# Two-layer Mamba, attention and experts kernel: another order of the start-up, one wider bias product, and a new table of half slots for layer 1

## The chip, the cores and the metric

The kernel runs on one core of a Trainium2 chip. The core has five engines with an instruction stream each: TensorE (PE), VectorE (DVE), ScalarE (ACT), GpSimd (POOL) and SyncE (SP), which mostly issues DMAs. They wait for each other through semaphores. The metric is the device time of one execution in microseconds (us); lower is better.

## The reference, cut to what matters

The input x is 32 sequences of 256 tokens with 128 features, float32. Two layers follow, each of the form x = x + attn(layernorm(x)) + ffn(layernorm(x)).

```python
# layer 0, attn: a Mamba block
xi, z = split(rmsnorm(xn, rms_w) @ in_proj)          # 128 -> 2 x 256
xi = silu(causal_conv4(xi, conv_w) + conv_b)
dt, Bm, Cm = split(xi @ x_proj)                      # 8, 16, 16
delta = softplus(dt @ dt_w + dt_b)                   # (tokens, 256)
h = exp(delta * A) * h + (delta * xi) * Bm           # scan over 256 tokens, 16 states
y = (sum(h * Cm) + xi * D) * silu(z);  attn = y @ out_proj
# layer 0, ffn: 8 experts, all computed, gated by top-p (0.8)
ffn = sum_e gate_e * (relu(xn @ W1[e] + b1[e]) @ W2[e] + b2[e])
# layer 1, attn: 16 heads, latent width 64, head width 8, rotary halves, causal softmax
q, k, v = ((xn @ W_down) per head) @ W_up;  attn = softmax(q k^T / sqrt(8)) v @ Wc
# layer 1, ffn: 128 experts, top 2, 32 places per expert, first come first served
```

## The kernel before, in words

Layer 0 (`layer0()`) works on 16 blocks of 512 tokens, each of 4 tiles of 128 tokens. A block is written as 32 half slots, h = 0 to 31, and every engine runs the same generic loop, `pipeline()` (L205). In each half slot an engine does the pieces of the current block (`slot`) and the pieces that prepare the next one (`fore`). Which `fore` piece stands in which half slot is read from a table for each engine (`PE_AT`, `ACT_AT` and so on, L181 to L187).

The pieces of the current block are these. ACT computes dA = exp(delta*A) (L555) from replicas of delta, which SP loads from DRAM into REP. POOL computes dBx (L685) from replicas of delta*x and of B (BC). DVE scans (L845) and multiplies with C (L854), and PE adds up the states (L395). Beside it PE computes the experts' up products (L374, bank UP) and down products (L383, bank DN); ACT applies relu (L564) and the gate (L571), and POOL sums (FF, L695). At the end of a block `output()` makes the experts' bias term (L405, from gT and b2) and the output projection (L407) in the bank FRO.

The pieces that prepare a block are XN and XQ on POOL (L734 to L742), the transposes (L442), the two conv halves x0 and x1 (L447, L451, then ACT L611, DVE L914), xproj (L458), the two halves of the delta input (L467, then ACT L597, L598), softplus (ACT L638, L642, L646; DVE L923, L933; POOL L751, L755), dx (POOL L762), the router (L479 and after) and z (L488). All of them use the one bank FRO. SP stores the results to the scratch tensors s_b, s_delta and s_dx and loads them back 32-fold (L261, L266).

Before block 0 the same pieces run alone, in one pass over 32 half slots (the prologue). There `between(s)` adds, once per slot of two half slots, the statistics of the remaining tiles of x (DVE L820), the products that combine layer 1's W_down and W_up (`project(n, part)`, n = q, k, v: PE L357 transposes and L362 products, ACT L527 to L537 copies), and, at its end, the layer norm of the other 60 tiles (`norms(OTHERS)`, DVE L993 to L1020 and L799 to L806, with two square roots on ACT, each of which loads a table). On SP the loads are issued in the order of the code: x (L244), 24 small loads (L248), x in six pieces (L251), four stores of a constant (L254), XI (L297), the experts' W (L314), the 21 loads for `project` (L316), b2 (L318).

Layer 1 (`layer1()`) is attention and the 128-expert part in one pipeline over the 32 sequences. A sequence has 12 half slots; `schedule()` puts each piece at its half slot 12n + at, or further ahead for the routing pieces (`ahead`), by the tables `PE_AT` to `SP_AT` (L1125 to L1129). The scores are computed twice: p1 (L1298 to L1310) gives row maxima (DVE `mx`, L1748), and p2 (L1320 to L1332) gives what ACT exponentiates (L1504); pv (L1346, L1348) multiplies with V. SP's `load` (L1208) issues 12 DMAs, KS and then QS, for the next sequence; it waits until p2 has read the old QS and until the parts of that sequence are stored. The routing pieces are g (L1387), `top` (DVE L1677, L1680), `mk`, `count` (L1401, L1402; ACT copy CS), `loc` (DVE L1694), `oh`, `val` and `map` (L1408). The output pieces are ot (L1448), `epi` (DVE L1731, L1733), yt (L1453), yT (ACT L1493) and wc (L1458). xnt (L1368) transposes the normed x, and xT (ACT L1477) copies it out.

Of the kernel before, what the change touches and what calls it, by code (L numbers as in the profile page):

```python
# [9 lines left out]
ALU = mybir.AluOpType  # L10
# [3 lines left out]
P = 128  # L14
# [36 lines left out]
def layer0(nc, ctx, t, dram, scratch):  # L51
# [19 lines left out]
    def sem(name):  # L71
# [3 lines left out]
    XC, XT = 6, (NT - J0) // 6  # L75
# [58 lines left out]
    wloaded = sem("wloaded"); dloaded = sem("dloaded"); wT = sem("wT"); wTc = sem("wTc"); wE = sem("wE"); stat_step2 = sem("stat_step2")  # L134
    root_done2 = sem("root_done2"); loaded = sem("loaded"); xloaded = [sem(f"xloaded{i}") for i in range(XC + 1)]; zeroed = sem("zeroed"); stat_step = sem("stat_step")
# [18 lines left out]
    a_log = dram["L0_attn_A_log"].rearrange("(b d) s -> d b s", d=CB)
# [3 lines left out]
    for h in range(HALF):  # L158

        rows = xproj[:, h, 0:2 * S].rearrange("p (a c q) -> p a c q", c=2, q=2)  # L160
        for c in range(2):
            loads.append((rows[:, :, c, :], xp[:, h, RANK + S * c:RANK + S * c + S].rearrange("p (a q) -> p a q", q=2)))
        loads.append((xproj[:, h, DT_AT:DT_AT + RANK], xp[:, h, 0:RANK]))
    wloads = [
# [11 lines left out]
    dloads = [(WD[:, n, :], dram[f"L1_attn_W{k}_down"]) for n, k in enumerate("qkv")]  # L176
# [11 lines left out]
    FIRST, OTHERS = slice(0, J0), slice(J0, NT)  # L188
    STATS_END = 2 * XC
    PROJ0 = 8  # L190
# [14 lines left out]
    def pipeline(fore, start, slot, end, eng, between=lambda s: None):  # L205
# [19 lines left out]
        start()  # L225
# [7 lines left out]
        end(IT0 - 1, 1)  # L233

# [7 lines left out]
    def _(sp):  # L242
        xd = tokens(dram["L0_attn_x"].rearrange("b t d -> (b t) d"))
        sp.dma_start(X0[:, 0:J0, :], xd[:, 0:J0, :]).then_inc(xloaded[0], 16)  # L244

        sp.wait_ge(zeroed, 1)
        for dst, src in loads:
            sp.dma_start(dst, src, allow_slow_non_contiguous=True).then_inc(loaded, 16)  # L248
        for g in range(XC):
            tiles = slice(J0 + g * XT, J0 + (g + 1) * XT)  # L250
            sp.dma_start(X0[:, tiles, :], xd[:, tiles, :]).then_inc(xloaded[g + 1], 16)  # L251
        for q in range(2):
            for k in range(HALF):
                sp.dma_start(seqs(d_d[q][k * P:(k + 1) * P, :])[:, :, 0:1], forget[:].unsqueeze(2), allow_slow_non_contiguous=True).then_inc(forgot, 16)  # L254
        for s in (xi_loaded, b_stored, d_stored, e_stored, *bc_loaded, *dr_loaded, *dx_loaded, xo_stored):
            sp.sem_inc(s.sem, 2 * s.per)

# [51 lines left out]
        def fore(h, n, q):  # L309
            start = isinstance(n, int) and n == 0  # L310
            if h == -EARLY and start:
                load_x(0)
                for dst, src in wloads:
                    sp.dma_start(dst, src, allow_slow_non_contiguous=True).then_inc(wloaded, 16)  # L314
                for dst, src in dloads:
                    sp.dma_start(dst, src, allow_slow_non_contiguous=True).then_inc(dloaded, 16)  # L316
                for j in range(J0):
                    sp.dma_start(b2[E0 * j:E0 * j + E0, j, :], dram["L0_ffn_b2"]).then_inc(wloaded, 16)  # L318
            elif h == SP_AT["bst"]:
                sp.wait_ge(dt_copied.sem, dt_copied.at(n, 1))  # L320
                sp.dma_start(b_d[q], dtB[0:2 * S, :]).then_inc(b_stored.sem, 16)
                if start:
                    load_x(1)
            elif h == SP_AT["dst"]:
# [3 lines left out]
            elif h == SP_AT["est"]:  # L328
# [4 lines left out]
                load_delta(0, n, q)  # L333
                load_dx(0, n, q)
            elif h == SP_AT["bc0"]:
# [5 lines left out]
    LOADED = 16 * len(loads)  # L341

    @block.tensor
    def _(pe):
        for s in (front, upf, downf, sumf, outf):
            pe.sem_inc(s.sem, 2 * s.per)
        pe.wait_ge(loaded, LOADED)
# [1494 lines left out]
```

## Time and profile before

| | us |
|---|---|
| median of 3 runs | 2269.92 |
| lowest and highest of them | 2262.42, 2271.96 |
| profiled execution | 2259.05 |
| span of its trace | 2257.3 |

| engine | busy us | share of the span |
|---|---|---|
| PE | 1991.2 | 88% |
| DVE | 1730.0 | 77% |
| ACT | 1340.6 | 59% |
| POOL | 1300.4 | 58% |

The profile is of the profiled execution, whose time is 1.75 us more than its span. It has four stages: the prologue of layer 0, until the first scan at 100.90 us; the 16 blocks, until about 1491 us; a transition, until layer 1's first p1 product at 1534.77 us; and layer 1. The share of busy time is an average over them. Engine times overlap, and what is idle on an engine that nobody waits for costs nothing. "[idle <-X]" behind a row says how long the engine had been idle and what it waited for.

### The profile page before, as it was taken

Reading aid. Unit: us, or ns where it says so; the run is one execution under the profiler, and the core shown is the slowest. Engines: PE = TensorE matmul, PEld = TensorE weight load, DVE = VectorE, ACT = ScalarE, POOL = GpSimd, SP = SyncE. Lnnn points to the kernel's source line nnn. Section 1 sums busy time; section 2 is a strip of 40 time slices with the busy share of each in tenths; the row PEclk is TensorE's granted clock in tenths of the full one; section 3 lists DMA queues with packets and bytes.
Section 4 is the critical chain, followed back from the end, with each engine's and each line's share of the span. In section 5 each row is a group of like instructions: output and inputs, shape, how many; then the busy total and the mean of one; then the engine's idle time right before and its main releaser. Section 6 shows DMA issues by size and latency. Waiting matters only on the chain. (4 is left out here: it accounts for less than half of the span.)

```text
span 2257.3 us, 40537 instructions
## 1 busy us (share of the span) xinstructions
PE 1991.2 (88%) x13714; PEld 1149.0 (51%) x13714; DVE 1730.0 (77%) x2778; ACT 1340.6 (59%) x2421; POOL 1300.4 (58%) x975
## 2 busy tenths in 40 slices
PE   1799999999999999999999999966899999987876
PEld 0455555555555555555555555533455555544442
DVE  3498888888888888888888898845777777765555
ACT  1576776776766767767767767622445554544443
POOL 0477867767767767778677687742332333324550
PEclk9999999999999999999999999967999999998897
DMA  7615505415325235145054153242222222234337
GB/s 193 137 38 111 127 26 132 102 47 130 85 63 132 68 85 132 46 107 131 22 132 104 42 131 92 46 117 88 84 91 80 85 82 86 85 109 113 114 115 230
DMA packets 184332, 222.49 MB, mean 99 GB/s; under 512 B 28488, under 2 KB 122736, under 8 KB 180016
## 3 DMA queue, kind: packets, MB, share of 16 engines
q1 hardware_dynamic: 182064, 215.52, 37.2%
q0 software_dynamic: 2048, 4.18, 0.7%
q8 instruction: 120, 1.97, 0.4%
q14 instruction: 100, 0.82, 0.1%
HBM read 165.41 MB, written 54.27 MB: 97 GB/s over the span
## 5 line engine op out<-in xcount | busy, mean ns | idle before, releaser
L685 POOL TENSOR_TENSOR dBx<-REP,BC 128x1024 f32<-128x1024 f32 x256 | 603.6, 2360 | 292.7 <-DVE dA L845 246.2
L845 DVE TENSOR_TENSOR_SCAN dA<-dA,dBx 128x512 f32<-128x512 f32 x512 | 626.6, 1224 | 117.4 <-ACT dA L555 66.4
L374 PE MATMUL UP<-xnT,W 128*128 128x512 f32 x1024 | 520.4, 628 | 53.9 <-ACT hT L564 41.8
L383 PEld LDWEIGHTS DN<-W,hT 128*128 128x128 f32 x4096 | 469.4, 192 | 108.6 <-issue 98.3
L383 PE MATMUL DN<-W,hT 128*128 128x128 f32 x4096 | 496.0, 278 | 0.3 <-ACT GD L571 0.3
L564 ACT ACTIVATE hT<-UP,b 128x512 f32<-128x512 f32 x512 | 355.8, 695 | 91.6 <-PE UP L374 84.4
L555 ACT ACTIVATE dA<-REP,A 128x512 f32<-128x512 f32 x512 | 354.3, 695 | 74.3 <-DVE PR L854 73.9
L854 DVE TENSOR_TENSOR PR<-dA,BC 128x512 f32<-128x512 f32 x512 | 353.4, 690 | 31.5 <-DVE dA L845 18.8
L1748 DVE TENSOR_REDUCE NM<-S 128x4 f32<-128x1024 f32 (+1 forms) x192 | 234.2, 1220 | 135.4 <-PE S L1310 88.3
L374 PEld LDWEIGHTS UP<-xnT,W 128*128 128x128 f32 x1024 | 181.6, 196 | 282.4 <-issue 146.5
L1504 ACT ACTIVATE PT<-S 128x1024 f32<-128x1024 f32 x192 | 196.8, 1025 | 111.8 <-PE S L1332 62.4
L571 ACT ACTIVATE GD<-DN,gate 128x128 f32<-128x128 f32 x512 | 145.8, 367 | 131.4 <-PE DN L383 130.6
L695 POOL TENSOR_TENSOR FF<-FF,GD 128x512 f32<-128x512 f32 x128 | 162.8, 1272 | 6.1 <-ACT GD L571 6.1
L395 PE MATMUL YS<-PR,fold 128*32 128x512 f32 x1024 | 138.0, 611 | 0.5 <-DVE PR L854 0.5
L1562 POOL TENSOR_TENSOR t<-t 128x512 f32<-128x512 f32 x32 | 40.6, 1268 | 126.2 <-DVE t L1672 126.2
L1485 ACT COPY CS<-ACC 128x256 f32<-128x256 f32 x64 | 23.8, 373 | 135.7 <-PE ACC L1402 135.7
L914 DVE SCALAR_TENSOR_TENSOR xch<-FRO,convw,xch 128x510 f32<-128x510 f32 (+2 forms) x96 | 71.5, 745 | 32.1 <-ACT xch L611 29.8
L1498 ACT COPY OSB<-OT 128x512 f32<-128x512 f32 x64 | 37.5, 586 | 87.8 <-PE OT L1348 86.2
L1298 PE MATMUL S<-maskq,identb 128*128 128x512 bf16 x128 | 42.5, 418 | 52.5 <-DMA QS<-s_parts 52.4
L1346 PE MATMUL OT<-PT,V 128*9 128x256 f32 x1024 | 87.5, 405 | 1.3 <-ACT PT L1504 1.3
L1577 POOL TENSOR_TENSOR OV<-OH,VAL 128x256 bf16<-128x256 bf16 x32 | 19.7, 614 | 112.5 <-DVE OH L1699 112.5
L1568 POOL TENSOR_TENSOR SPL<-t,SPL 128x512 bf16<-128x512 f32 x32 | 37.1, 1159 | 73.2 <-ACT SPL L1510 73.0
(246 smaller groups left out, 2819.7 us busy)
## 6 DMA issues: line engine op xcount, KB each, us to landing
REP<-s_delta SPq DMA_DIRECT2D x128, 256.0 KB, 8.2
REP<-s_dx SPq DMA_DIRECT2D x128, 256.0 KB, 7.4
BC<-s_b SPq DMA_DIRECT2D x128, 256.0 KB, 8.6
s_parts<-SPL SPq DMA_DIRECT2D x32, 384.0 KB, 2.8
s_dx<-tz SPq DMA_DIRECT2D x16, 512.0 KB, 3.1
s_y<-zeros SPq DMA_DIRECT2D x32, 256.0 KB, 5.3
YC<-s_y SPq DMA_DIRECT2D x16, 512.0 KB, 5.1
s_delta<-soft SPq DMA_DIRECT2D x32, 255.0 KB, 2.7
```

The lines of the kernel that those rows point to most:

```text
L374: nc.tensor.matmul(UP[k % 2][:], W1[:, e % E0, f * P:(f + 1) * P], xnT[:, q, :], start=True, stop=True).then_inc(upf.sem, 1)
L383: last = nc.tensor.matmul(DN[:, j * P:(j + 1) * P], hT[:, e % 2, f, j * P:(j + 1) * P], W2[:, e, f, :], start=(f == 0), stop=(f == FB - 1))
L395: last = nc.tensor.matmul(YS[CB * j:CB * j + CB, :], fold[:], PR[:, (DB * b + j) % (2 * DB), :], start=(q == 0), stop=(q == NQ - 1), tile_ ...
L555: nc.scalar.activation(dA[:, k % 3, :], DR[:, h, j, :], ACT.Exp, scale=A[:, h, j, q:q + 1]).then_inc(da_ready.sem, 1)
L564: nc.scalar.activation(hT[:, e % 2, f, :], UP[k % 2][:], ACT.Relu, bias=b1[:, e % E0, f:f + 1]).then_inc(relu_done.sem, 1)
L571: last = nc.scalar.activation(GD[:, e % 2, j, :], DN[:, j * P:(j + 1) * P], ACT.Copy, scale=gate[:, par, j, e:e + 1])
L685: nc.gpsimd.tensor_tensor(dBx[:, s % 2], DX[:, h, j:j + 2, :], BC[:, q // 2, q % 2, :].unsqueeze(1).to_broadcast([P, 2, T0]), ALU.mult).th ...
L695: nc.gpsimd.tensor_tensor(FF[:, par], FF[:, par], GD[:, e % 2], ALU.add).then_inc(acc_done.sem, 1)
L845: nc.vector.tensor_tensor_scan(h, h, dBx[:, k // 2 % 2, k % 2, :], 0.0, ALU.mult, ALU.add).then_inc(scan_done.sem, 1)
L854: nc.vector.tensor_tensor(PR[:, k % (2 * DB), :], dA[:, k % 3, :], BC[:, q // 2, 2 + q % 2, :], ALU.mult).then_inc(prod_done.sem, 1)
L1504: nc.scalar.activation(PT[:, u // 3, u % 3, :], S2[:].rearrange("p b w -> p (b w)"), ACT.Exp, scale=SCALE).then_inc(exp_done.sem, 1)
L1748: nc.vector.tensor_reduce(NM[:, 0 if a == 0 else 1, :].rearrange("p (r i) -> p r i", r=2)[:, :, heads], S1[:].rearrange("p r (j k) -> p r ...
```

## The change

**Layer 0's start-up.** XI, the input of block 0, is loaded behind the first x load, which is twice as long; only five small loads (`first_loads`) are awaited before block 0's first products, the next ten follow on SP, and nine more and the four constants are issued by ACT. The three W_down loads and the 18 small W_up loads come next, then x in seven pieces, then the experts' W. The scaling of the weights is split in two (prep, prep2). In block 0 the second of each pair of products goes to the bank DN instead of FRO (`bank()`). `project()` stands earlier for n = 0, the statistics are made in other slots, and the layer norm of the other tiles (now 56) is moved from the prologue into block 0, at half slots 8, 12 and 15, with its square roots at 9 and 13. SP loads the replicas for block 0 in half pieces (`begin()`), and the first exp and dBx wait for the first of these. PE and POOL make the first up products and dBx at half slots 27 and 28.

PE's stream at the start, before (XQ is the normed input, dA and YS the banks of `project`):

```order
L442 MATMUL FRO<-ident,XQ 128x128 x3
L447 MATMUL FRO<-xrT,inproj 128x512 [waits xT_copied]
L451 MATMUL FRO<-xrT,inproj 128x512 [waits conv_step]
L458 MATMUL FRO<-xi,xproj 40x512 [waits x_done,conv_step,xi_done]
L458 MATMUL FRO<-xi,xproj 40x512
L467 MATMUL FRO<-dtB,dtw 128x512 [waits dt_copied]
L467 MATMUL FRO<-dtB,dtw 128x512 [waits u_done]
L473 MATMUL FRO<-ident,XN 128x128 [waits u_done,xn_ready]
L473 MATMUL FRO<-ident,XN 128x128 x3
L357 MATMUL dA<-ident,hT 128x128 [waits dloaded]
L357 MATMUL dA<-ident,hT 128x128 x7
```

The same place now:

```order
L473 MATMUL FRO<-ident,XQ 128x128 x3
L478 MATMUL FRO<-xrT,inproj 128x512 [waits xT_copied]
L483 MATMUL DN<-xrT,inproj 128x512
L386 MATMUL dA<-ident,hT 128x128 [waits downs]
L386 MATMUL dA<-ident,hT 128x128 x7
L392 MATMUL YS<-PR,hT 128x32 [waits wTc,dloaded]
L392 MATMUL YS<-PR,hT 128x32 x7
L386 MATMUL dA<-ident,hT 128x128 [waits wTc,downs]
L386 MATMUL dA<-ident,hT 128x128 x7
L492 MATMUL FRO<-xi,xproj 40x512 [waits conv_step,x_done,xi_done,loaded]
L501 MATMUL FRO<-dtB,dtw 128x512 [waits dt_copied]
L501 MATMUL DN<-dtB,dtw 128x512
```

The second conv half and the second delta half no longer wait, and three groups of `project` stand ahead of xproj.

**Output.** The four bias products of 128 columns, each ahead of its two output products, become one of 512 columns. PE, end of a block, before:

```order
L405 MATMUL FRO<-b,gT 128x128
L407 MATMUL FRO<-outproj,y 128x128 x2
L405 MATMUL FRO<-b,gT 128x128
L407 MATMUL FRO<-outproj,y 128x128 x2
L405 MATMUL FRO<-b,gT 128x128
L407 MATMUL FRO<-outproj,y 128x128 x2
L405 MATMUL FRO<-b,gT 128x128
L407 MATMUL FRO<-outproj,y 128x128 x2
```

The bias products have 32 rows of weights and the output products 128, so before the kind changes eight times in a block, and now twice. The sum of the same four terms is unchanged.

**Layer 1.** Only the tables change. PE's half slots 2 and 3 of a sequence in the steady part, between the last two pv groups (names as above; EP<-ident,YN is yt and FR<-ident,XN is xnt), before:

```order
L1330 MATMUL S<-QS,KS 128x256 x4
L1332 MATMUL S<-maskk,identb 128x2x128 x2
L1368 MATMUL FR<-ident,XN 128x128 x2
L1453 MATMUL EP<-ident,YN 128x128 x2
L1308 MATMUL S<-KS,QS 128x256 x4
L1310 MATMUL S<-maskq,identb 128x2x128 x2
L1401 MATMUL ACC<-MK,tri 128x256
L1402 MATMUL ACC<-CS,last_row 128x256
```

The same place now:

```order
L1383 MATMUL S<-QS,KS 128x256 x4
L1385 MATMUL S<-maskk,identb 128x2x128 x2
L1361 MATMUL S<-KS,QS 128x256 x4
L1363 MATMUL S<-maskq,identb 128x2x128 x2
L1454 MATMUL ACC<-MK,tri 128x256
L1455 MATMUL ACC<-CS,last_row 128x256
```

And PE's rows from the end of the pv group behind it (OT is pv's bank, EP<-wc,yT is wc), where the last L1385 is what SP's next load of QS waits for:

```order
L1399 MATMUL OT<-PT,V 9x256
L1401 MATMUL OT<-PT,V 9x128
L1511 MATMUL EP<-wc,yT 128x128 x2
L1383 MATMUL S<-QS,KS 128x256 x4
L1385 MATMUL S<-maskk,identb 128x2x128 x2
L1421 MATMUL FR<-ident,XN 128x128 x2
```

xnt and yt have left the half slots ahead of that L1385, and wc has come in.

The core of the diff:

```diff
+                for dst, src in first_loads:
+                    sp.dma_start(dst, src, allow_slow_non_contiguous=True).then_inc(needed, 16)
+                for dst, src in loads[:10]:
+                    sp.dma_start(dst, src, allow_slow_non_contiguous=True).then_inc(loaded, 16)
+                for dst, src in down_loads:
+                    sp.dma_start(dst, src, allow_slow_non_contiguous=True).then_inc(downs, 16)
...
+    STATS_AT = {2: (0,), 4: (1,), 5: (2,), 6: (3,), 7: (4,), 8: (5, 6)}
+    NORMS_AT, ROOTS_AT = (8, 12, 15), (9, 13)
+    PE_PROJ = {2: ((0, 0),), 3: ((0, 1), (1, 0)), 10: ((1, 1), (2, 0)), 13: ((2, 1),)}
+    START_AT = 27
...
+    def bank(n, k):
+        return DN if k == 1 and isinstance(n, int) and n == 0 else FRO
...
+        def begin(n, q):
+            sp.wait_ge(d_stored.sem, d_stored.at(n, 16 * HALF))
+            sp.wait_ge(forgot, 2 * HALF * 16)
+            for j in range(0, DB, 2):
+                for rep, src, first, loaded in ((DR, d_d[q], begun, dr_loaded), (DX, e_d[q], begun_x, dx_loaded)):
+                    if j == 0 and rep is DX:
+                        sp.wait_ge(e_stored.sem, e_stored.at(n, 16))
+                    for r in range(NQ):
+                        rows = src[0:P, :].rearrange("(j d) t -> d j t", d=CB)[:, j:j + 2, :]
+                        sp.dma_start(rep[CB * r:CB * r + CB, 0, j:j + 2, :], rows).then_inc(first if j == 0 else loaded[0].sem, 16)
...
+            nc.tensor.matmul(FRO[:], gT[:, par, :], b2[:].rearrange("p j d -> p (j d)"), start=True, stop=False)
             for j in range(J0):
-                nc.tensor.matmul(FRO[:, j * P:(j + 1) * P], gT[:, par, :], b2[:, j, :], start=True, stop=False)
...
+            if first and h in NORMS_AT:
+                norms(OTHERS, NORMS_AT.index(h), stat_step2, root_done2)
...
-    PE_AT = dict(xnt=-23, g=-16, count=(-13, -10), map=-3, qk=-20, rot=-18, v=-3, p1=0, nmt=12, p2=17, pv=(21, 24, 26, 30), ot=(32, 34), yt=37, wc=41)
-    ACT_AT = dict(xT=-21, cs=(-12, -9), v=-1, spl=(-15, -12), nm=14, exp=18, osb=(26, 32), yT=41)
-    DVE_AT = dict(top=-15, mk=-13, loc=(-11, -8), oh=-7, add=-2, t1=-18, t2=-15, mx=1, nms=12, epi=(34, 37), x=42)
-    POOL_AT = dict(norm=-23, keep=-14, val=-6, qk=-15, r1=-13, spl=-11)
-    SP_AT = dict(xn=-13, parts=-8, load=-7, nm=12, nm_in=16, we=-16)
+    PE_AT = dict(xnt=-21, g=-17, count=(-13, -10), map=-3, qk=-20, rot=-18, v=-3, p1=0, nmt=12, p2=17, pv=(21, 24, 26, 30), ot=(32, 34), yt=35, wc=38)
+    ACT_AT = dict(xT=-20, cs=(-12, -9), v=-1, spl=(-15, -12), nm=13, exp=18, osb=(26, 32), yT=39)
+    DVE_AT = dict(top=-15, mk=-13, loc=(-11, -9), oh=-8, add=-2, t1=-18, t2=-15, mx=1, nms=12, epi=(34, 35), x=42)
+    POOL_AT = dict(norm=-23, keep=-13, val=-5, qk=-15, r1=-13, spl=-11)
+    SP_AT = dict(xn=-14, parts=-11, load=-6, nm=12, nm_in=15, we=-17)
```

## Rows read from the trace of the kernel before

**Rows 1.** Page, parts 4, 5, 6: chain by engine line; two groups; one load of replicas.

```profile
DMA QS<-s_parts 7%; SPq L1208 7%; PE OT L1346 2%; PE S L1330 1%; PE S L1298 1%; PE S L1332 1%; PE ACC L1402 1%; PE OT L1348 1%; PE S L1308 1%; DVE NM L1748 1%; PE S L1310 1%; DMA YC<-s_y 1%; PE S L1302 1%; PE FR L1387 0%; PE FR L1379 0%
...
L1748 DVE TENSOR_REDUCE NM<-S 128x4 f32<-128x1024 f32 (+1 forms) x192 | 234.2, 1220 | 135.4 <-PE S L1310 88.3
...
L1504 ACT ACTIVATE PT<-S 128x1024 f32<-128x1024 f32 x192 | 196.8, 1025 | 111.8 <-PE S L1332 62.4
...
REP<-s_dx SPq DMA_DIRECT2D x128, 256.0 KB, 7.4
```

**Rows 2.** Windows by stage: start:end, length, busy time, PEclk, DMA share, GB/s.

```profile
0.00:100.90 100.90, 41.33 (x121) 24.02 (x122) 35.17 (x134) 28.98 (x43) 23.64 (x28) 0.95 0.69 172
...
100.90:1490.70 1389.80, 1311.67 (x7009) 773.32 (x7007) 1203.43 (x1432) 969.46 (x1815) 1017.79 (x651) 0.98 0.38 87
...
1534.77:1695.05 160.28, 135.86 (x1266) 76.19 (x1266) 116.34 (x340) 64.96 (x113) 49.21 (x70) 0.92 0.27 85
...
1695.05:2011.60 316.55, 293.08 (x3136) 163.91 (x3136) 225.15 (x564) 163.08 (x258) 96.27 (x111) 0.99 0.27 86
...
2011.60:2257.30 245.70, 191.41 (x2125) 100.81 (x2125) 131.25 (x238) 106.54 (x177) 90.60 (x87) 0.86 0.48 142
```

**Rows 3.** Timeline, first 101 us: start, length, engine, line, [idle before <-releaser].

```profile
8.73 0.16 DVE L806 TENSOR_TENSOR q<-rrms,rstd 128x4 f32<-128x4 f32 x1
...
28.60 0.37 SPq L297 DMA_DIRECT2D XI<-in_L_attn_x  x1
...
32.12 1.03 POOL L734 TENSOR_TENSOR XN<-XI,mean 128x512 f32<-128x512 f32 x1 [29.91 <-DMA XI<-in_L_attn_x]
...
50.18 3.63 PE L458 MATMUL FRO<-xi,xproj 128*40 128x512 f32 x4 [6.27 <-DVE xi L919]
...
57.99 2.07 PE L467 MATMUL FRO<-dtB,dtw 8*128 8x512 f32 x2 [1.44 <-ACT soft L598]
...
72.89 2.35 POOL L762 TENSOR_TENSOR tz<-soft,xi 128x1024 f32<-128x1024 f32 x1
...
100.90 1.23 DVE L845 TENSOR_TENSOR_SCAN dA<-dA,dBx 128x512 f32<-128x512 f32 x1 [10.00 <-ACT dA L555]
```

**Rows 4.** Timeline, first 101 us: prices of single steps.

```profile
47.76 1.88 SPq L316 DMA_DIRECT2D PR<-in_L_attn_Wk_up_e  x3
...
62.38 1.91 PE L357 MATMUL dA<-ident,hT 128*128 128x128 f32 x8
...
67.61 3.60 PE L362 MATMUL YS<-PR,hT 128*128 128x32 f32 x16
...
81.85 0.26 DVE L993 TENSOR_TENSOR q<-stats 128x60 f32<-128x60 f32 x1
...
83.29 1.28 ACT L514 ACT_TABLE_LOAD   x1
...
89.42 0.22 DVE L806 TENSOR_TENSOR q<-rrms,rstd 128x60 f32<-128x60 f32 x1
```

**Rows 5.** Timeline of PE, 199 to 210 us: output() of one block.

```profile
198.81 3.84 PE L383 MATMUL DN<-W,hT 128*128 128x128 f32 x32
...
204.30 0.48 PE L405 MATMUL FRO<-b,gT 32*128 32x128 f32 x2
...
204.71 0.71 PE L407 MATMUL FRO<-outproj,y 128*128 128x128 f32 x4
...
208.43 1.88 PE L374 MATMUL UP<-xnT,W 128*128 128x512 f32 x4
```

**Rows 6.** Waits of POOL, 500 to 1350 us: total, times, longest.

```profile
POOL dBx L685 <- DMA BC<-s_b: 25.0, 9, 3.7
```

**Rows 7.** Waits of PE, 1534 to 1695 us.

```profile
PE ACC L1408 <- issue: 9.4, 10, 1.0
...
PE ACC L1408 <- DVE junk L1694: 3.8, 2, 1.9
```

**Rows 8.** Waits of PE, 1695 to 2011 us.

```profile
PE S L1298 <- DMA QS<-s_parts: 18.9, 16, 1.7
```

More of the change, by code:

```diff
@@ L203, in place, with pipeline @@
         return k // (NQ * DB), k // DB % NQ, k % DB
-    def pipeline(fore, start, slot, end, eng, between=lambda s: None):
+    def pipeline(fore, start, slot, end, eng, between=lambda s: None, start_at=START_AT):
         def iteration(it, par, **kind):
@@ L243, in _ @@
         xd = tokens(dram["L0_attn_x"].rearrange("b t d -> (b t) d"))
[L244 to L254, printed above, removed]
         for s in (xi_loaded, b_stored, d_stored, e_stored, *bc_loaded, *dr_loaded, *dx_loaded, xo_stored):
             sp.sem_inc(s.sem, 2 * s.per)
+        sp.dma_start(X0[:, FIRST, :], xd[:, FIRST, :]).then_inc(xloaded[0], 16)
         def load_rep(rep, src, h, loaded):
@@ L332, in fore @@
                     sp.wait_ge(stat_step2, 1)
-                load_delta(0, n, q)
-                load_dx(0, n, q)
-            elif h == SP_AT["bc0"]:
+                    begin(n, q)
+                else:
+                    load_delta(0, n, q)
+                    load_dx(0, n, q)
+            elif h == SP_AT["bc0"] and not start:
                 load_states(0, n, q)
@@ L448, in fore @@
             if h == PE_AT["x1"]:
-                pe.wait_ge(conv_step.sem, conv_step.at(n, 3))
-                nc.tensor.matmul(FRO[:], inproj[:, P:2 * P], xrT[:], start=True, stop=True).then_inc(front.sem, 1)
+                if bank(n, 1) is FRO:
+                    pe.wait_ge(conv_step.sem, conv_step.at(n, 3))
+                nc.tensor.matmul(bank(n, 1)[:], inproj[:, P:2 * P], xrT[:], start=True, stop=True).then_inc(front.sem, 1)
             if h == PE_AT["xproj"]:
+                if isinstance(n, int) and n == 0:
+                    pe.wait_ge(loaded, LOADED)
                 pe.wait_ge(xi_done.sem, xi_done.at(n, 1))
@@ L495, in between @@
         def between(s):
-            if PROJ0 <= s < PROJ0 + 6:
-                project((s - PROJ0) // 2, (s - PROJ0) % 2)
+            for n, part in PE_PROJ.get(s, ()):
+                project(n, part)
         def end(it, par):
@@ L539, in between @@
         def between(s):
-            if PROJ0 <= s < PROJ0 + 6:
-                project((s - PROJ0) // 2, (s - PROJ0) % 2)
-            if s == STATS_END:
-                roots(OTHERS, stat_step2, root_done2)
+            for n, part in ACT_PROJ.get(s, ()):
+                project(n, part)
+            if s == PREP_AT:
+                act.wait_ge(loaded, LOADED)
+                nc.scalar.activation(A[:], A[:], ACT.Exp).then_inc(aexp, 1)
         LAST_IN_BANK = {0: -1, 1: 0, 2: -2}
@@ L592, in slot @@
                 apply_gate(s // 2, it, par)
+            if first and h in ROOTS_AT:
+                root(OTHERS, ROOTS_AT.index(h), stat_step2, root_done2)
         def delta_input(k, n):
             act.wait_ge(front.sem, front.at(n, 5 + k))
-            nc.scalar.activation(umax[:, k, :], FRO[:], ACT.Relu, bias=dtb[:, k:k + 1])
-            nc.scalar.activation(soft[:, k, :], FRO[:], ACT.Abs, bias=dtb[:, k:k + 1]).then_inc(u_done.sem, 1)
+            nc.scalar.activation(umax[:, k, :], bank(n, k)[:], ACT.Relu, bias=dtb[:, k:k + 1])
+            nc.scalar.activation(soft[:, k, :], bank(n, k)[:], ACT.Abs, bias=dtb[:, k:k + 1]).then_inc(u_done.sem, 1)
         def fore(h, n, q):
@@ L766, in fore @@
                 tri = tri8[:].rearrange("p (e o) -> p e o", o=E0).unsqueeze(1).to_broadcast([P, J0, E0, E0])
+                if isinstance(n, int) and n == 0:
+                    pool.wait_ge(loaded, LOADED)
                 pool.wait_ge(gate_step.sem, gate_step.at(n, 7))
```

179 lines of the change are left out of this document (103 added, 76 removed).

## The prediction

> **What bounds the kernel now.** I read the windows by stage first, then the chain of waits, then each stage's timeline and waits. In the windows [rows 2] the reader is to see three regimes. In the prologue, until the first scan, PE is busy for 41.33 of 100.90 us: a chain of single steps through all engines, which nothing overlaps. In the 16 blocks PE is busy for 1311.67 of 1389.80 us, so a microsecond taken from PE there is worth up to a microsecond. In layer 1 PE is busy for 135.86 of 160.28, then 293.08 of 316.55, then 191.41 of 245.70 us. The windows are cut at the p1 products of sequences 0, 7 and 23, so a sequence takes 160.28 / 7 = 22.9 us and then 316.55 / 16 = 19.8 us. The chain gives its largest shares to the load of QS and to SP's issue of it [rows 1]: in the middle stage the next sequence waits for the last one's p2, twelve issues and the landing. PE waits there only 18.9 us in 16 times [rows 8], as the ring and PE are nearly in balance.
>
> **Start-up, the front.** XN, the first step of block 0, starts at 32.12 us and waits for XI, which was issued at 28.60 [rows 3]: XI needs about 3.5 us and is simply late in SP's queue. Now it is SP's second DMA, so the norms of the first tiles release XN. They ended at 8.73 + 0.16 us [rows 3]; twice the tiles are loaded (256 KB more, about 1 us at 172 GB/s / 0.69 = 249 GB/s [rows 2]) and four more statistics made (about 0.9). XN at 11.0: -21.1.
>
> From XN to xproj it was 50.18 - 32.12 = 18.1 us. With x1 in a second bank the second conv starts as the first ends; I take 3 us off (one product of two passes and one tap that stood between). So xproj could start at 26. But three groups of `project` now stand ahead of it on PE, and the second of them waits for 18 small loads. Three such issues took 1.88 us [rows 4], 18 take 11.3; with 20 DMAs ahead of them at 0.4 to 0.6 each [rows 3, 4] they are issued by about 23 and land at about 26. Then 3.60 us for the 16 passes of L362 and 1.91 for L357 [rows 4]: xproj at 31.5, so the move gives back 5.5 of the gain. From xproj to the end of dx it was 72.89 + 2.35 - 50.18 = 25.1; the second delta product waited 1.44 us and is now right behind the first [rows 3], -2.0 with its issue, and the router's first DVE step goes behind the logarithm's, -0.9. So 22.2, and dx ends at 53.7 (before: 75.2).
>
> **Start-up, the back.** From dx to the first scan it was 100.90 - 75.24 = 25.7 us [rows 3]. Inside lay the norms of 60 tiles, from 81.85 to 89.64 [rows 4], on which POOL, and so the first dBx, depended, and whole replicas. Now: store of dx about 3, half pieces of the replicas (a whole load lands 7.4 us after issue [rows 1]; halves 4 to 6), dBx 2.4: scan at about 65. The loads of x and W behind them are 7.9 MB, at 249 GB/s 32 us from about 23, so done at about 55; that they delay the small stores is the risk. I take 65 in a range of 61 to 74: -36.
>
> What left the prologue comes back in block 0: the norms take DVE about 5 of the 7.8 us, and two square roots with a table of their own cost ACT four loads of 1.28 us [rows 4]. Block 0 is no fuller than the others, but its DVE and ACT feed the scan: +4.5, between 0 and 10. Start-up in all: **-31.5**, from -40 to -18.
>
> The Trainium skill (DMA: Bandwidth & Descriptors, Issuing engines are not separate DMA queues) says that all issuers share the same 16 DMA engines and that issuing from several saves only sequencer time. By it the 13 DMAs that went to ACT save their issue alone; the trace's DMA share of 0.69 in this stage agrees that the engines are no free resource here. The sum stays as it is.
>
> **Output.** In the rows of one block [rows 5], the two passes of a bias product take from 204.30 to 204.71 = 0.41 us and the next four output passes take 0.64 (four such pairs end at 208.43: 4.13 us). Elsewhere a pass of 128 columns costs 3.84 / 32 = 0.12 and one of 512 columns 1.88 / 4 = 0.47. By these, 0.41 is 0.24 + 0.17 and 0.64 is 0.48 + 0.16: each change between 32 and 128 rows costs about 0.17. Now there are two passes of 0.47, sixteen of 0.12 and two changes: 0.94 + 1.92 + 0.34 = 3.2. That saves 0.93 us in each of 16 blocks, 14.9. PE is the fullest engine, but in some blocks POOL waits for BC (25.0 us in 9 times [rows 6]), and what the slowest of the four engines does there isn't PE's. I take **-14**, from -18 to 0.
>
> The Trainium skill speaks on both sides here. TensorEngine Tiling (Array Packing), Key Properties, says that changing the tiling mode drains TensorE; the trace agrees, with 0.17 us for each change. TensorE: Matmul & The Clock Gate, in its section on LDWEIGHTS, says that a 32x128 load of weights takes as long as a 128x128 one; by columns alone the old form would be 24 x 0.12 = 2.9 us and the new one 2.9, and nothing would be saved. The trace's 4.13 speaks against it.
>
> **Layer 1.** No instruction is added or removed; pieces change places. In the early stage PE waits ahead of map (L1408) for 9.4 us in 10 times and for 3.8 in 2 [rows 7], 13.2 / 7 = 1.9 us a sequence. The releaser is DVE's `loc` and what follows it, which stood behind a maximum of 1.2 us [rows 1] and now stands ahead of it. Against that the copy of xnT (ACT) comes later for v, about 0.5, and the loss of the gap behind xnt. Five or so periods: -8, between -13 and 0. At its start the parts leave about 1 us sooner: -1. In the middle stage the ring decides. xnt and yt (four passes) leave the half slots before the last p2, wc (four passes) comes in: the same count, but wc waits for yT, a copy on ACT behind an exp; +0.1 for each of 16, and +0.3 for each of the 8 later ones: +3 in all. **-6**, from -16 to +8.
>
> **Sum.** -31.5 - 14 - 6 = -51.5. Against the profiled execution, 2259.05 - 51.5 = 2207.5; the median of the runs shown is 2269.92, 10.9 above that execution, and by it I get 2218.4. I say 2217, as the median is what will be compared. About 0.5% (11.3 us) is what a measurement of this kernel can tell from no change.
>
> **Rivals.**
> 1. The front of the prologue is early, but its back isn't: s_delta, s_dx and the replicas queue behind x and W on the same DMA engines (0.69 busy already [rows 2]), and the first up products wait for W, which now comes last. First scan at 80: 15 us less gain, 2232. For it: 7.9 MB. Against it: they should be through before the replicas are asked for.
> 2. The output saving is swallowed: a block then lasts as long as its ring through POOL, DMA and DVE, which doesn't get shorter. For it: the wait on BC [rows 6], nearly one in each block. Against it: PE's 94% in that stage. Or the product costs by its columns. Gain 0 there: 2231.
> 3. Layer 1 gains nothing early, and wc costs the ring 1 us in each of some 16 sequences: +20 against my term, 2237. The early gap may be filled by another wait of the same length.
> 4. All three together: about -2, no change that can be told.
> 5. Slower. wc waits in the ring of each sequence for yT behind two exps of ACT, 2 x 1.025 us [rows 1], in all 31: +64 instead of -6, so +18: 2288. It decides from about 1.5 us a sequence on. For it: the ring has no slack (QS waits [rows 8]) and wc is three half slots earlier. Against it: yT and `epi` are moved earlier too, by 2 half slots on ACT.
>
> **How the numbers follow.** Forecast 0.57, rival 1 0.12, rival 2 0.15, rival 3 0.09, rival 4 0.03, rival 5 0.04. The forecast's own range by its terms is 2195 to 2240 (two of the three terms don't fail together often). Rivals 1 to 3 lie within 2231 to 2237, or a little above where my sizes are off too; the range is 2192 to 2243 and leaves out 4, 5 and the far ends. Faster: forecast and rivals 1 to 3, 0.93; same 0.03; slower 0.04.
>
> **What would show it.** XN at about 11 us (if not before 15, the first step is wrong); xproj near 31, with a wait of PE for the small loads ahead of it; dx done near 54; first scan near 65; the first block longer than the others by some 5 us. In output() about 3.2 us between the last down product and the next up product, and a period of the blocks about 0.9 shorter. In layer 1 early periods near 21 instead of 22.9 and no wait ahead of map; middle periods of 19.8 to 20.0, with the chain through QS as before. I am wrong if the first scan comes after 75, the blocks' period stays, or the middle period goes over 20.5.

## The result, and the profile after

The changed kernel takes 2214.76 us (median of 4 runs, 2212.37 to 2217.88); the kernel before takes 2267.56 (4 runs, 2262.42 to 2271.96). The ratio is 0.9764, with a 95% interval of 0.9737 to 0.9791: 47 to 60 us less. The forecast was 2217.

The two profiled executions differ by only 2257.3 - 2216.1 = 41.2 us of span. Where they lie is seen in the windows of the new trace, cut at the first scan, at the first scans of blocks 1 and 15, and at the p1 products of sequences 0, 7 and 23 (the first and the last three are cuts of [rows 2] too). The columns are start:end, length, busy time of PE, weight loads, DVE, ACT and POOL, PEclk, DMA share and GB/s.

```profile
0.00:74.35 74.35, 37.91 (x120) 23.89 (x121) 31.44 (x111) 26.19 (x40) 21.39 (x27) 0.76 0.83 205
74.35:162.66 88.31, 80.95 (x415) 46.32 (x413) 81.19 (x107) 69.33 (x124) 61.40 (x40) 0.97 0.43 98
162.66:1367.57 1204.91, 1136.75 (x6085) 662.20 (x6084) 1063.50 (x1274) 862.04 (x1610) 907.06 (x586) 0.98 0.40 93
1491.30:1637.45 146.15, 131.78 (x1268) 77.04 (x1268) 119.45 (x342) 65.89 (x114) 49.95 (x70) 0.94 0.29 93
1637.45:1955.97 318.52, 292.36 (x3137) 165.39 (x3137) 226.94 (x562) 162.71 (x257) 88.43 (x111) 0.99 0.27 85
1955.97:2216.00 260.03, 202.52 (x2123) 104.51 (x2123) 131.60 (x238) 105.99 (x177) 90.18 (x86) 0.84 0.46 134
```

| stage | before | changed | difference | forecast |
|---|---|---|---|---|
| to the first scan | 100.9 | 74.35 | -26.5 | -36 |
| block 0 | 83.6 | 88.3 | +4.7 | +4.5 |
| blocks 1 to 14, each | 87.55 | 86.07 | -1.48, -20.8 in all | -0.93 |
| block 15 and transition | 124.6 | 123.7 | -0.9 | -2 |
| layer 1, sequences 0 to 6 | 160.3 | 146.15 | -14.1 | -8 |
| sequences 7 to 22 | 316.6 | 318.5 | +2.0 | +1.6 |
| sequence 23 to the end | 245.6 | 260.0 | +14.4 | +2.4 |

The last row is not the change: two experiments with layer 1's old tables (a1 and a4 below) have 261.7 and 264.0 us there, and of all fourteen profiles only before and d1 (240.8) are below 260. The profiled execution of before was a short one in this stage. Its time, 2259.05, is 8.5 us below its kernel's median, and that of the changed kernel, 2217.88, is 3.1 above its own; that is why the medians differ by 52.8 us and the two spans by 41.2. Why the stage was short is not shown. In the middle row old tables give 312 (a4) to 317 us and the new ones 316 (a3) to 321 (b6), so a difference of one pair of profiles there is uncertain by some 4 us.

### The profile page after: what moved, and what is told of

The parts are those of the page before. It is cut to its first block and busy times, and to the rows that moved or that the text cites. A ratio compares the mean times of both kernels' runs of the same rounds, so it can differ in the third digit from the quotient of the medians.

```text
span 2216.1 us, 40363 instructions
## 1 busy us (share of the span) xinstructions
PE 1973.5 (89%) x13618; PEld 1134.9 (51%) x13618; DVE 1736.0 (78%) x2778; ACT 1343.3 (61%) x2423; POOL 1293.1 (58%) x975
## 5 line engine op out<-in xcount | busy, mean ns | idle before, releaser
L906 DVE TENSOR_TENSOR PR<-dA,BC 128x512 f32<-128x512 f32 x512 | 353.6, 691 | 31.5 <-DVE dA L897 18.8
L1748 DVE SCALAR_TENSOR_TENSOR junk<-iota,ef,ACC 128x128 bf16<-128x128 f32 x128 | 39.2, 344 | 53.8 <-ACT CS L1538 53.8
```

What stands on the lines that cost most here:

```text
L906: nc.vector.tensor_tensor(PR[:, k % (2 * DB), :], dA[:, k % 3, :], BC[:, q // 2, 2 + q % 2, :], ALU.mult).then_inc(prod_done.sem, 1)
```

## The start-up in the new trace

The timeline of the changed kernel's first 75 us, against [rows 3] (start, length, engine, line, operation, idle before and its releaser):

```profile
12.90 1.07 POOL L781 TENSOR_TENSOR XN<-XI,mean 128x512 f32<-128x512 f32 x1 [10.69 <-DVE q L859]
...
29.44 1.65 DVE L873 BATCH_NORM_STATS2 stats<-REP 128x6 f32<-128x128 f32 x8 [4.50 <-DMA REP<-in_L_attn_x]
...
31.00 1.21 DVE L973 SCALAR_TENSOR_TENSOR xi<-th,xch 128x1024 f32<-128x1024 f32 x1
...
32.31 3.22 PE L492 MATMUL FRO<-xi,xproj 128*40 128x512 f32 x4 [0.43 <-issue]
...
40.12 12.01 SPq L344 DMA_DIRECT2D b<-in_L_ffn_b  x4
...
49.39 2.35 POOL L809 TENSOR_TENSOR tz<-soft,xi 128x1024 f32<-128x1024 f32 x1
...
52.18 0.32 SPq L347 DMA_DIRECT2D s_b<-dtB  x1
...
56.05 1.99 SPq L270 DMA_DIRECT2D BC<-s_b  x4
...
58.09 1.25 SPq L354 DMA_DIRECT2D s_delta<-soft  x2
59.38 0.65 SPq L357 DMA_DIRECT2D s_dx<-tz  x1
...
65.62 1.75 SPq L295 DMA_DIRECT2D REP<-s_delta  x4
...
69.70 1.30 ACT L597 ACTIVATE dA<-REP,A 128x512 f32<-128x512 f32 x2 [7.68 <-DMA REP<-s_delta]
...
74.35 1.23 DVE L897 TENSOR_TENSOR_SCAN dA<-dA,dBx 128x512 f32<-128x512 f32 x1 [17.92 <-POOL dBx L732]
```

XN starts at 12.9, xproj at 32.3 and dx ends at 51.7 us; forecast were 11, 31.5 and 53.7. So the front came out as the sum said. But dx is stored only at 59.4, and the scan follows 15 us later. Four tiny loads of b2 (4 KB each) hold SP for 12 us, from 40.12 to 52.13. Only then does s_b go out; SP waits 3 us for it to land, issues BC, and s_delta and s_dx come behind that. The windows of the same trace show the moved bytes:

```profile
30.00:35.00 5.00, 4.57 (x13) 2.07 (x12) 5.00 (x23) 1.75 (x4) 0.00 (x0) 0.50 1.15 346
...
45.00:50.00 5.00, 5.00 (x23) 4.78 (x23) 2.33 (x5) 1.71 (x5) 3.84 (x4) 0.50 1.06 341
50.00:55.00 5.00, 4.34 (x20) 2.66 (x18) 3.11 (x5) 2.49 (x5) 3.86 (x4) 0.79 1.02 285
```

The DMA share (last but one column) is above 1 in these stretches (0.99 over the whole stall): x and W keep the DMA engines full while SP stands, and it goes on as their bytes run out. How much the queue holds, no run shows. Before, SP stood as long behind the same bytes:

```profile
33.39 10.21 SPq L316 DMA_DIRECT2D hT<-in_L_attn_Wq_down  x1
```

But there the stall fell on the first load for `project`, and it was over at 43.6 us, before s_b's input was ready (54.4).

## Experiments

Each was run beside the kernel before on one chip; the ratio is to that kernel, with its 95% interval.

**a1_output_only.** The kernel before with

```diff
+nc.tensor.matmul(FRO[:], gT[:, par, :], b2[:].rearrange("p j d -> p (j d)"), start=True, stop=False)
 for j in range(J0):
-    nc.tensor.matmul(FRO[:, j * P:(j + 1) * P], gT[:, par, :], b2[:, j, :], start=True, stop=False)
     (the output products as before; the stop flag stands at the last one alone)
```

> The kernel before, with only the one 512-column bias product in output(). Theory (each change between 32 and 128 rows of weights costs PE about 0.17 us, and PE is what bounds a block): 0.93 to 1.2 us less in each of 16 blocks, so 15 to 20 us less than before, ratio 0.991 to 0.994; the block period in the trace falls from 87.5 to about 86.5. Rival (the period is set by the ring through POOL, DMA and DVE, and the 20 us that the blocks of the changed kernel gained came from its other phase after the new start-up): below 5 us, period 87.2 or more.

Ratio 0.9938 (0.9915 to 0.9961): 2253.3 against 2269.6, 16 us less. The period of the blocks is 86.04 us, that of the changed kernel. So the gain of the blocks is output()'s and doesn't depend on the start-up.

**a2_output_back.** The changed kernel with these lines reversed.

> The changed kernel with the four bias products of 128 columns put back. Theory: +15 to +20 us against the changed kernel (2214.8), so about 2232, period of the blocks 87.5. Rival (the blocks gained by their phase after the start-up): less than 8 us more.

2236.7, ratio 0.9857 (0.9830 to 0.9884) against 0.9764: 21 us more, period 87.26. The rival falls from this side as well.

How far a single period can be trusted is seen over all profiles. The eleven kernels of this document with one bias product of 512 columns have periods of 85.82 (b6) to 86.61 us (d1), 86.17 in the mean; the two with four products, 87.55 and 87.26. The means differ by 1.2 us.

**a3_output_two.** The changed kernel with

```diff
+for g in range(2):
+    nc.tensor.matmul(FRO[:, 2 * g * P:2 * (g + 1) * P], gT[:, par, :], b2[:, 2 * g:2 * g + 2, :]..., start=True, stop=False)
+    (the four output products of tiles 2g and 2g + 1)
```

> The changed kernel with two bias products of 256 columns, each ahead of its four output products: the same columns, four changes of row count in a block instead of two (before: eight). Theory of the changes: output() takes 2 x 0.17 = 0.34 us more a block than in the changed kernel (2.94 there), 3.3, and the kernel +5 us. Rival (number of bias instructions, at a fixed cost of 0.3 for each beyond the first): 3.25, the same here; rival by columns alone: 2.94, no change.

PE's timeline in one block of the changed kernel, and then of this one, from the first bias product to the next up product:

```profile
182.44 1.12 PE L434 MATMUL FRO<-b,gT 32*128 32x512 f32 x2
183.49 2.05 PE L437 MATMUL FRO<-outproj,y 128*128 128x128 f32 x16
185.38 1.88 PE L404 MATMUL UP<-xnT,W 128*128 128x512 f32 x4
```

```profile
182.76 0.69 PE L435 MATMUL FRO<-b,gT 32*128 32x256 f32 x2
183.39 1.16 PE L438 MATMUL FRO<-outproj,y 128*128 128x128 f32 x8
184.47 0.69 PE L435 MATMUL FRO<-b,gT 32*128 32x256 f32 x2
185.10 1.16 PE L438 MATMUL FRO<-outproj,y 128*128 128x128 f32 x8
186.09 1.88 PE L404 MATMUL UP<-xnT,W 128*128 128x512 f32 x4
```

output() takes 2.94 us in the one and 3.33 in the other, 4.13 before, in each of the first 15 blocks: 2, 4 and 8 changes of the row count with the same columns, 0.2 us for each change. By columns alone all three would be equal, so that is out. A fixed cost of each bias instruction gives 0.39 us for the second and 0.40 for each of the next two, so by these totals it fits as well: in all three forms each bias product brings two changes. The single passes tell more. The first ones of output() before, each from the timeline of a narrow window of its own:

```profile
204.30 0.37 PE L405 MATMUL FRO<-b,gT 32*128 32x128 f32 x1
...
204.51 0.27 PE L405 MATMUL FRO<-b,gT 32*128 32x128 f32 x1
...
204.71 0.38 PE L407 MATMUL FRO<-outproj,y 128*128 128x128 f32 x1
...
204.93 0.50 PE L407 MATMUL FRO<-outproj,y 128*128 128x128 f32 x3
```

The two bias passes and the first output pass each take 0.20 to 0.22 us until the next one starts. The second and the third output pass take 0.11, and the last one before the next bias product takes 0.20 again. So each bias product brings four gaps that are 0.1 us too long, two around each change. One of the four lies between the first two output passes, behind the bias product; a price of the bias instruction alone doesn't explain that one. PE's weight loads show the same: inside a run a load starts 0.11 us ahead of its pass, and at a change together with it.

The period of the blocks, 86.94, is 0.8 us above the mean of those with one product, where PE's rows give 0.39; but this is one profile, and the others differ by as much among themselves. The kernel takes 2223.1 us (0.9791, 0.9768 to 0.9814); by the ratios that is 6 us more than the changed kernel, what 16 times 0.39 gives, and the intervals overlap.

**a4_l1_tables_back.** The changed kernel with layer 1's five old tables.

> The changed kernel with layer 1's old tables. Theory (the tables gain 14 us in sequences 0 to 6, lose 2 in 7 to 22 and 14 in 23 to 31, as the two profiles differ): the total within 5 us of the changed kernel, early stage near 160 us, last stage near 246. Rival (the last stage's 14 us are chance: clock and code loading of that one execution): old tables cost +8 to +14 in all, and the last stage comes out between 246 and 260 in either kernel.

2225.3, ratio 0.9814 (0.9789 to 0.9839): 10.6 us more than the changed kernel, so the tables gain some 11. The theory, with a total within 5 us, was wrong. The rival is right in that the last stage's 14 us are no effect of the tables, though 264.0 is above its 246 to 260. The three stages of layer 1 in this kernel, and the last one of a1:

```profile
1486.15:1645.97 159.82, 134.15 (x1266) 75.95 (x1266) 116.07 (x340) 64.86 (x113) 49.18 (x70) 0.93 0.27 85
1645.97:1958.36 312.39, 290.05 (x3137) 162.71 (x3137) 225.25 (x566) 163.26 (x258) 96.32 (x111) 1.00 0.27 87
1958.36:2222.40 264.04, 199.65 (x2125) 104.39 (x2125) 128.41 (x238) 105.74 (x177) 90.53 (x87) 0.84 0.45 132
```

```profile
1983.28:2245.00 261.72, 198.62 (x2125) 103.87 (x2125) 127.44 (x238) 105.97 (x177) 90.48 (x87) 0.84 0.46 133
```

Against this kernel the new tables gain 13.7 us early, lose 6.1 in the middle (between 0 and 8 by all the profiles) and change nothing sure at the end. This kernel also gives the start-up its price: it differs from a1 in layer 0's start-up alone, ran on the same chip, and takes 28.0 us less (2225.3 against 2253.3). PE's waits ahead of map (`ACC`) in the early stage of this kernel, and the only such row that is left in the changed one:

```profile
PE ACC L1461 <- issue: 9.4, 10, 1.0
PE ACC L1461 <- DVE junk L1748: 3.9, 2, 2.0
```

```profile
PE ACC L1461 <- DVE junk L1748: 1.5, 2, 0.7
```

**b1_w_from_act.** W, b1 and b2 issued by ACT at slot 2 of the prologue, not by SP.

```diff
+            if s == 2:
+                for dst, src in wloads:
+                    act.dma_start(dst, src, allow_slow_non_contiguous=True).then_inc(wloaded, 16)
+                (and the four b2 loads)
```

> The changed kernel, with the experts' W, b1 and the four b2 loads issued by ACT (after its copies of project(0,0), at about 23 us) instead of SP. In the changed kernel SP stands at the b2 loads from 40.12 to 52.13 us, and s_b, s_delta and s_dx go out at 52.2, 58.1 and 59.4 although dx was done at 51.7. Theory (SP's own queue is full behind x and W): SP gets past at once, s_delta goes out near 49.5, s_dx near 52, and the first scan comes at 65 to 68 instead of 74; total 6 to 9 us less than the changed kernel. Rival (the DMA engines are what is full): the stall is as long wherever the loads are issued, scan at 74, no gain, or later because x and the small loads are delayed by W.

The rival is right: 2230.4, ratio 0.9831 (0.9808 to 0.9855), first scan at 74.78. Now both queues stand:

```profile
25.63 21.94 SPq L340 DMA_DIRECT2D REP<-in_L_attn_x  x7
...
27.11 13.63 ACTq L580 DMA_DIRECT2D b<-in_L_ffn_b  x4
...
61.62 2.35 POOL L810 TENSOR_TENSOR tz<-soft,xi 128x1024 f32<-128x1024 f32 x1
```

ACT, which makes the tanh of block 0, is held until 40.7, and dx ends 12 us later than in the changed kernel. That the first scan is nevertheless hardly later says that most of those 12 us were slack. The kernel takes 15.6 us more than the changed one all the same, by its median; its profiled execution, the shortest of the four, is only 5.5 us longer, and most of that lies in layer 1. Where the rest is, is not shown.

**b2_project_late** and **b3_project_stats_late.** `PE_PROJ` and, in the same way, `ACT_PROJ` change in both, `STATS_AT` in the second only:

```diff
-    PE_PROJ = {2: ((0, 0),), 3: ((0, 1), (1, 0)), 10: ...
+    PE_PROJ = {2: ((0, 0),), 9: ((0, 1), (1, 0)), 10: ...
-    STATS_AT = {2: (0,), 4: (1,), ...
+    STATS_AT = {4: (0, 1), ...
```

> The changed kernel, with project(0,1) and project(1,0) moved from slot 3 to slot 9 of the prologue, behind xproj and the delta products. The prediction had it that these two put xproj back by 5.5 us. Theory by the new trace: xi on DVE stands behind the statistics of the first x piece, which wait for it until 29.4, so xproj stays near 32 without the two as well, and dx moves by less than 1.5 us; SP's stall hides even that: first scan within 1 us of 74. Rival (PE's order was the cause): xproj at 27, dx 5 us earlier.

> As the last, with the first piece of statistics also moved, from slot 2 to slot 4. Theory: xi at about 26 and xproj at 27.5, dx done 4 to 5 us earlier (about 47), but s_delta still goes out after SP's stall, at 58, so the first scan stays within 1.5 us of 74. Rival: the first scan follows dx, 69 to 70.

2221.2 (0.9794, 0.9761 to 0.9827) and 2215.6 (0.9752, 0.9733 to 0.9771); first scans at 72.41 and 73.82. Two rows of the first, then two of the second:

```profile
29.35 1.64 DVE L873 BATCH_NORM_STATS2 stats<-REP 128x6 f32<-128x128 f32 x8 [4.81 <-DMA REP<-in_L_attn_x]
...
32.22 3.61 PE L492 MATMUL FRO<-xi,xproj 128*40 128x512 f32 x4 [10.57 <-DVE xi L973]
```

```profile
27.49 3.60 PE L492 MATMUL FRO<-xi,xproj 128*40 128x512 f32 x4 [4.84 <-DVE xi L973]
...
47.98 2.35 POOL L809 TENSOR_TENSOR tz<-soft,xi 128x1024 f32<-128x1024 f32 x1
```

With `project` out of its way PE waits 10.57 us for xi and xproj stays at 32.2: what held xi was DVE's statistics of a piece of x that had not landed. With those moved too, xproj comes 4.8 us earlier but dx, done at 50.3, only 1.4, and the scan doesn't move. The delta products took 2.07 and 1.91 us there, at a granted clock of 0.50 (the lower level), and 1.12 and 1.02 at 1.00 in the changed kernel; before they took 2.07 at a recorded 1.00, so the recorded clock doesn't explain all of it. Of the expectations the readings of xi and xproj held, and the scan didn't follow dx. Those of dx did not: 1.7 us later instead of within 1.5 in b2, and not 4 to 5 earlier in b3. The first scan of b2 is also 1.9 us before the changed kernel's. But the five profiles with the changed kernel's own start-up (it, a2, a3, a4 and c1) have first scans from 72.21 to 74.35, and a difference inside that is none.

**b4_one_bank.** `bank()` returns FRO always.

> The changed kernel with all products of block 0's front in FRO again (x1, dt1, z1 wait for the bank). The prediction gave 3 us to x1 and 2 to dt1. Theory by the new trace: x1's 3 us are hidden behind the load of the first x piece, dt1's 2 us reach dx (dx done at 53 to 54 instead of 51.7), and SP's stall until 58 hides them: first scan within 1 us, total within 3. Rival: 5 us later.

2218.1 (0.9765, 0.9744 to 0.9786), first scan at 73.42, dx done at 53.5. As expected: the second bank, worth 5 us in my sum, is worth 1.8 us at dx and none that can be told in the time (3.4 us by the medians, none by the ratios).

**b5_bias_loads_late** and **b6_bias_project_stats_late.** The four b2 loads moved behind `begin(n, q)`; the second with b3's lines as well.

> The changed kernel with only the four b2 loads moved, from ahead of s_b to behind the replicas of block 0 on SP. In the changed kernel these four take SP 12.0 us, about 3 each, as its queue drains. Theory (each DMA issued behind x and W waits for room, some 3 us for each, until about 52): s_b takes the first place (out at 43), BC the next, and s_delta and s_dx go out at about 50 to 52 instead of 58 to 59.4: first scan at 67 to 70, total 4 to 7 us less than the changed kernel. Rival (SP's queue is blocked as a whole until the W loads are through, whatever comes next): s_b still at 52, s_delta at 58, scan at 74, no gain.

> The last one with project(0,1), project(1,0) and the first statistics late as well, so that dx is done at about 50.3. Theory: SP's stall decides, so it equals the last one within 1.5 us in its first scan. Rival: dx decides once SP is free, 1.5 us or more earlier than the last one.

2218.7 (0.9774, 0.9744 to 0.9804) and 2219.1 (0.9784, 0.9755 to 0.9813); first scans at 73.13 and 72.45. My theory of one place for each 3 us was wrong. A row of the first:

```profile
40.20 10.31 SPq L345 DMA_DIRECT2D s_b<-dtB  x1
```

The first DMA behind W stands, whichever it is, until some 50.5 us (the four b2 loads until 52.1). That the second equals the first within 1.5 us (0.7) held, but tells little, as neither freed SP.

**c1_l1_output_pieces_back.** The changed kernel with the output pieces at their old half slots:

```diff
-PE yt=35, wc=38   ACT yT=39   DVE epi=(34, 35)   (the rest of the tables stays)
+PE yt=37, wc=41   ACT yT=41   DVE epi=(34, 37)
```

> The changed kernel with yt, wc, yT and the second epi back at their old half slots (37, 41, 41, 37); the routing pieces (xnt, g, loc, oh, keep, val, xT) and SP's stay as changed. Theory (early gain by the routing pieces, middle loss by wc and epi in the Q ring): early stage 146 to 155 as in the changed kernel, middle stage 312.5 (as with all old tables) instead of 316 to 318, so 3 to 5 us less than the changed kernel. Rival (the middle loss comes from the routing pieces or SP's order): middle stage 316 or more, total within 2 us.

2208.9 (2205.0 to 2210.8), ratio 0.9739 (0.9717 to 0.9761), 5.9 us less than the changed kernel, with intervals that overlap; the stages say more. Early and middle stage:

```profile
1488.76:1632.62 143.86, 128.90 (x1267) 75.23 (x1267) 117.40 (x337) 64.24 (x113) 49.94 (x70) 0.96 0.29 94
1632.62:1941.56 308.94, 286.93 (x3136) 164.62 (x3137) 228.26 (x567) 163.09 (x258) 87.53 (x111) 1.00 0.28 88
```

PE's waits in the middle stage, of the changed kernel and then of this one (total, times, longest):

```profile
PE S L1351 <- DMA QS<-s_parts: 27.4, 17, 3.8
```

```profile
PE S L1351 <- DMA QS<-s_parts: 10.8, 16, 1.2
PE S L1361 <- DVE NM L1802: 9.7, 16, 0.6
```

The early stage keeps the whole gain, so the output pieces have no part in it. It belongs to the routing pieces or to SP's slots and ACT's `nm`, which moved together; no run parts them. The middle stage is 9.6 us shorter than in the changed kernel, and 308.9 here and 307.9 in d1, which has the same tables, lie below all others: the moved output pieces cost 0.6 us a sequence. The Q ring is a part of that: PE's two waits together are 20.5 us instead of 27.4. Another is PE's own products, 286.93 instead of 292.36 us at a granted clock of 1.00 instead of 0.99. Against all old tables (a4) the stage is 3.5 us shorter, so these gain there too.

**d1_stores_from_act.** c1, with block 0's s_b, s_delta and s_dx issued by ACT.

```diff
...
+                        if isinstance(n, int) and n == 0:
+                            for i in range(HALF):
+                                act.dma_start(seqs(d_d[q][i * P:(i + 1) * P, :])[:, :, 1:], seqs(delta[:, i, :])[:, :, 1:]).then_inc(d_stored.sem, 16)
+                            act.wait_ge(dx_done.sem, dx_done.at(n, 1))
+                            act.dma_start(e_d[q].rearrange("(h p) t -> p h t", p=P), dx[:]).then_inc(e_stored.sem, 16)
 (s_b alike, behind ACT's copy of dtB; the same three taken out of SP's stream for block 0)
```

> The last kernel (c1: the changed kernel with layer 1's output pieces back; 2208.9, first scan at 73.4), with block 0's three stores s_b, s_delta and s_dx issued by ACT instead of SP, whose queue stands until 50 to 52 us behind x and W. Theory (SP's own queue is what holds the stores, and after it the wait on them): s_b goes out at 36, s_delta near 50, s_dx near 52, so SP can issue BC and the replicas at once when it is free, at 53 to 56 instead of 65: first scan at 64 to 67, total 6 to 9 us less than c1, near 2201. Rival (the DMA engines themselves are behind by then): the stores land no earlier than 60, first scan 72 to 74, no gain. ACT's three issues cost it about 1.5 us in either case.

2189.7 against 2250.9 for the kernel before, which was quicker on this chip than on the others: ratio 0.9717 (0.9689 to 0.9746). It is the best of all by its ratio, but its interval overlaps c1's. Rows of its trace:

```profile
50.02 0.64 ACTq L708 DMA_DIRECT2D s_delta<-soft  x1
51.53 0.40 ACTq L710 DMA_DIRECT2D s_dx<-tz  x1
...
57.41 1.73 SPq L295 DMA_DIRECT2D REP<-s_delta  x4
...
66.83 1.30 ACT L599 ACTIVATE dA<-REP,A 128x512 f32<-128x512 f32 x2 [2.63 <-DMA REP<-s_delta]
...
71.21 1.23 DVE L907 TENSOR_TENSOR_SCAN dA<-dA,dBx 128x512 f32<-128x512 f32 x1 [15.02 <-POOL dBx L742]
```

The stores go out 8 us earlier and the replicas are asked for 8.2 us earlier than in the changed kernel (7.1 earlier than in c1), somewhat later than expected; but from there to the first exp it is 9.4 us instead of 4.1 (65.62 to 69.70 in the changed kernel), and the scan gains 2.2 us against c1 instead of 6 to 9. That is 1.0 us below the earliest of the five profiles with the old order, so even this gain is barely clear. The trace shows where the rest went. The stores, issued while W was still coming in, took 7 us to land. The replicas' half pieces took 7.2 us instead of 2.9 to 3.3, with a DMA share of 1.11 and 1.00 in the windows 55 to 60 and 60 to 65 us (0.79 and 0.74 in c1). By then W had landed, as its first products ran at 57.6: what the replicas shared the engines with was mainly BC and their own second pieces. So both theories hold a part: SP's order held the stores, but with that out of the way the stores and the loads took longer on full engines.

## Why the prediction was right, and where its steps were off

- **What bounds each stage** held: PE is busy for 37.9 of 74.35 us in the start-up, for 94% of the blocks and for 90% and 92% of layer 1's first two stages.
- **Start-up, the front**: right in its end (dx at 51.7, forecast 53.7), partly by luck. XN was 1.9 us late, and from xproj to the end of dx it took 19.4 us instead of 22.2. xproj came at the forecast time, but b2 shows that the step "the move gives back 5.5" named the wrong holder: the statistics of a late x piece held xi as long. The 3 us of the second bank lay under that wait, and b4 shows that the other 2 reach dx and not the scan.
- **Start-up, the back**: the step that failed is "scan at about 65". From dx to the scan it took 22.6 us, not 11. Two terms account for most of it. A wait of dx's store for SP was put at nothing and was 7.6 us (51.74 to 59.38): the stall until 52.1, the landing of s_b, and the issues of BC and s_delta. The stores, put at about 3 us, took 6.2 (s_delta) and 7.4 (s_dx) to land, so the replicas were asked for 6.2 us after s_dx went out. The half pieces of s_dx and dBx came out as forecast, at 4.5 and 2.4, behind 1.8 for the issues of s_delta's. It is rival 1's mechanism at 9 of its 15 us; my sum had W's bytes drained at 55 (right) and treated them as no obstacle for the stores in SP's queue (wrong: b5, d1). The first scan, 74.35, is 0.35 beyond the end of my bound, and the latest of the five profiles with this start-up; their mean is 73.2.
- **Block 0 longer by 4.5**: measured 4.7, and 3.1 (d1) to 5.4 (b2) in the experiments. I did not try the norms and the table loads alone.
- **Output -14**: by a1 16.3 us, by a2 21. The price of a change, 0.17 us, came out as 0.20, and output() was 1.19 us shorter, not 0.93. The period fell by 1.5 in the pair of profiles and by 1.2 in the means over all kernels, so PE's saving came through whole (rival 2 is out).
- **Columns alone**: the three forms differ with the same columns, 4.13, 3.33 and 2.94 us, so this is out. The Trainium skill (TensorE: Matmul & The Clock Gate, LDWEIGHTS) says that a 32x128 load of weights takes as long as a 128x128 one; the trace agrees, with 181 to 184 ns for the loads of the bias product and 186 to 192 for those of the output products in the block shown. So the cost is not in the length of a load. The Trainium skill (TensorEngine Tiling (Array Packing), Key Properties) says that a change of tiling mode drains TensorE; the loads that start late at each change, and the even steps of the three forms, agree with it, though no run shows a drain as such.
- **Layer 1 -6**: by a4 -10.6. The early term was mis-sized, -14 instead of -8: of the 13.2 us that PE waited ahead of map [rows 7] 1.5 are left, and nothing came in their place at v; PE's own products are 2 to 4 us shorter there too. The middle term, +1.6, is +2 to +6: the wait for QS rose from 18.9 [rows 8] to 27.4 us, rival 3's mechanism at a third of its price. c1 shows both signs apart. The sum itself had a slip: 0.1 for each of 16 and 0.3 for each of 8 sequences are +4, not +3.
- **The sum** met the time by luck: in the profiles the start-up, with block 0, gained 9.7 us less than forecast, and 6.8 more in the blocks and some 5 in layer 1 made up for it. By the medians, where the start-up gained 28.0 (a4 against a1), it was 3.5 less, with 2 to 7 more for the output and 5 more in layer 1. The terms were each within a factor of two.

## What to carry to other kernels

A DMA queue that takes bulk loads ahead of small, urgent stores is a wait that no engine's busy share shows: count the bulk's bytes against the time at which the small ones are due. Moving one of them to another queue helps little while the engines are full: of the 7 to 8 us by which the stores went out earlier in d1, the scan kept about 2. Before crediting a shortened step, find what else releases the same instruction: here three edits to the front (second bank, order of products, order of statistics) each moved dx by less than 2 us, and the scan by nothing that can be told. When a table of slots has several edits, split it by what the pieces feed: one part of this one gained and another lost.

## What the runs showed of the hardware

Behind some 8 MB of queued loads of x and W an issue stood for 10.3 us on SP (b5), and four stood for 13.6 us on ACT (b1), while the engines moved 323 and 317 GB/s at a DMA share of 1.00 and 1.02. A change between passes with 32 and with 128 rows of weights cost PE 0.2 us (a3). In layer 1's last stage the same code took 261.6 us in c1 and 240.8 in d1, at a mean granted clock of 0.85 and 0.88; PE's busy time for it was 199.1 and 188.8 us, so half of the difference lies in its products. Since d1 ran on a chip where the kernel before was quicker too (2250.9 us against 2269.0), single profiles from different chips can differ by some 20 us here with no change of code.
